# A selective-scan stage whose state input comes by broadcast DMA in place of selecting matmuls

## The chip, the cores and the metric

The kernel runs on one core of one Trainium2 chip. The metric is device time in microseconds of one execution; the times shown are those of three runs. One further execution was taken with the hardware profiler, and all rows below are from it. The engines are named as in the profile: PE is TensorE (PEld its weight loads), DVE is VectorE, ACT is ScalarE, POOL is GpSimd, SP is the engine that issues the DMAs.

## The reference

Two layers work on x, 8 sequences of 256 tokens with 128 features. Layer 0 adds grouped attention (16 heads, 4 key/value heads) and an expert layer with a softmax gate to x. Layer 1 adds a selective-scan block and a gated feed-forward block to the result, both from the same normalised input. The part that the change touches is the scan block:

```python
xz = x @ W_in
xs, z = (xz[..., :d_inner], xz[..., d_inner:])
...
xs = jax.nn.silu(xc.transpose(0, 2, 1))
dt = jax.nn.softplus(xs @ W_dt + b_dt)
Bs = xs @ W_x
A_exp = jnp.exp(A_log)
def step(h, inp):
    dt_t, Bs_t, x_t = inp
    h = h * jnp.exp(-A_exp[None] * dt_t[..., None]) + Bs_t[:, None, :]
    return (h, jnp.sum(h, axis=-1) + D * x_t)
...
y = ys.transpose(1, 0, 2) * jax.nn.silu(z)
return y @ W_out
```

There are 256 channels (two tiles of 128 partitions), 16 states per channel, and sequences of 256 tokens. For a state s, the state input Bs is one row of tokens that is the same for all channels; the decay differs by channel.

## The kernel before

Tokens lie along the free dimension in layer 1. The 2048 tokens are four groups (g = 0 to 3) of 512, each two sequences. Every engine has an order written out by hand (`ORDERS`): a list of pieces, each with the waits that it needs, which the engine runs from first to last. Layer 0 and layer 1 are interleaved in these lists.

For one group of layer 1 the pieces are:

- `x_transposes` and `x_out`: the normalised rows are transposed on TensorE and copied by ScalarE. `normalise` makes them on ScalarE in two passes per row tile (lines 997 and 1001).
- `x_in` (line 889): four matmuls, two for the x half and two for the z half, all into banks `pA` and `pB`. The z half waits for the convolution of the x half to leave the banks. `taps`, `conv` (line 1101, three multiply-adds per channel tile on VectorE), `gate_x` and `xm` (line 1092) make xs; `gate_z` and `zm` make z's gate.
- `start_acc` (line 988): ScalarE starts the accumulator with D times xs.
- `wx` (line 897): the state input, 16 rows three times over in 96 partitions. ScalarE copies it out twice (lines 1013 and 1014), and GpSimd's `split` turns it into three bf16 parts (lines 1178 to 1184).
- `b` (`b_row`, line 825): for each state one bf16 matmul with a selecting matrix brings its row to all 128 partitions, into a PSUM bank (bank 2 or 3).
- `dt` and `D` (`decay`, line 1047): ScalarE makes the step size, and for each state and channel tile the decay, into a ring of 31 SBUF tiles.
- `scan` (line 1125): for each state and channel tile one scan on VectorE. It reads the decay from SBUF and the state input from the PSUM bank and writes `hb`, eight SBUF tiles (four states by two channel tiles).
- `add` (line 1165): GpSimd adds each `hb` tile to the accumulator. `y` (line 1173) multiplies it by z's gate. A scan waits until the adds of four states before are done.
- `ffn`, `mul`, `second`, `gelu`, `third`, `hid`: the feed-forward block, TensorE and ScalarE with products on VectorE (lines 1081 and 1084).
- `out` (lines 925 and 927): the output rows of both blocks, into `pB`; `residual1` (line 1132) adds them to x, and SP writes the group out (line 805).

In all there are 4 groups by 16 states by 2 channel tiles: 128 scans and 128 adds. The scan reads its two operands like this (lines 1125 to 1127):

```python
eng.tensor_tensor_scan(hb[:, s % NPAIR, c, :],
                       da(n).rearrange("p b n -> p (b n)"),
                       b_bank(g, s)[:, :], 0.0, ALU.mult, ALU.add).then_inc(scan, 1)
```

In layer 0, `normalised` (line 631) is a `tensor_scalar` on VectorE; `G` on GpSimd (lines 680 to 699) is the gate's arithmetic on small tiles; `first_split` on VectorE (lines 639 to 645) splits the first sequence's queries and keys, and line 645 subtracts one SBUF tile from another. `warm` (line 445) is a matmul on constant data that keeps TensorE occupied.

Of the kernel before, what the change touches and what calls it, by code (L numbers as in the profile page):

```python
# [50 lines left out]
     ("alog", (CI, NS)), ("D", (CI,)), ("bdt", (CI,)), ("pick", (NS,))),  # L51
# [14 lines left out]
def settled(eng, sem, v):  # L66


    eng.wait_ge(sem, v)
# [3 lines left out]
    sync="""3*x_in constants0 head ffn_weights 3*put fetch stack 3*put fetch stack 3*put loads fetch 3*rows loads 3*put  # L73
        fetch 3*rows loads stack 2*put 2*rows put rows stack fetch loads 3*put 3*rows fetch stack 3*put 3*rows
        fetch stack 3*put 3*rows stack fetch 3*rows stack 3*rows 4*out landed""",
    tensor="""36*warm xn_transposes 4*warm project v_gate ffn_in 11*warm ffn_in 3*warm xn_transposes ffn_out 3*warm
        project ffn_in 2*S 2*warm xn_transposes S ffn_in S project S ffn_out 2*S 8*warm S xn_transposes warm S
        warm S 2*warm S warm S warm S 3*warm S 2*warm S 5*warm 2*S 4*warm max_rows warm S warm v_gate S warm S
        project warm 2*S 3*warm S A 2*warm S 2*A 2*S A S A S A pv S A S A ffn_in A S A S pv ffn_in A S A S
        max_rows ffn_out A S v_gate A S pv A S A S A S A pv S A S A heads A S A S pv A back xn_transposes A S A  # L80
        S proj_out project A S A S pv 2*S A ffn_in A S max_rows A pv v_gate ffn_in S A S A ffn_out S A S A pv S
        A S A heads S A S A pv xn_transposes A S A S back project S A S A pv proj_out S A S ffn_in 2*A S
        max_rows ffn_in S A S A pv v_gate S A S ffn_out A S A S pv A S A S heads A S A pv S A xn_transposes A S
        back project A S A S proj_out ffn_in 2*S A pv A S A ffn_in S A max_rows A ffn_out S A S v_gate pv S A S
        A pv S A S A heads A S A S pv A back A S xn_transposes proj_out A S A S project 2*A S pv S A S A pv S
        max_rows S ffn_in S A S v_gate A S ffn_in 2*S pv A S A S heads ffn_out S back A S A S proj_out S 2*A S
        pv 2*A 2*S A S A pv S 2*A max_rows ffn_in pv A 2*S A v_gate ffn_in A 2*S A ffn_out A S A S pv A S A S
        heads S A S A pv x_transposes A S A S back x_in S A S A pv proj_out ffn 2*A x_in max_rows A pv A ffn
        2*x_in 2*A ffn wx A pv ffn heads 2*step_in back b A second x_transposes proj_out A second b second A
        x_in b A x_in second b A pv A x_in A x_in A pv A b A wx A b step_in pv step_in b 2*A b 2*A b pv b second  # L90
        heads second 2*b 2*second b back third proj_out third b third b third b third b 2*third b x_transposes
        third b 2*x_in 2*ffn 2*b 2*x_in ffn wx b ffn b 2*out b step_in 2*second b 3*second 2*b second out b out
        second b x_transposes second b step_in b third b x_in third b 2*third x_in b 2*third b x_in 2*third b
        ffn b ffn b x_in wx b 2*ffn out b out step_in 2*out b 2*second b second b second b second b 2*second b
        second b step_in b third b third b 2*third b third b third b third b third b ffn b ffn out b out b 2*ffn
        b 2*out b 5*second 2*b 3*second b 3*third b 5*third 4*out""",
    scalar="""roots 3*deviation0 xn_out qk_out gate_exp 2*relu xn_out qk_out relu xn_out relu qk_out negated_maxima xn_out
        gate_exp qk_out 8*E relu 2*E relu E negated_maxima 7*E o_out 2*E gate_exp 3*E xn_out 2*E qk_out 3*E
        decay_rates negated_maxima relu 2*E relu 4*E o_out E gate_exp 3*E xn_out 2*E qk_out 3*E relu 2*E
        negated_maxima relu 5*E o_out 2*E gate_exp 3*E xn_out E qk_out 2*E relu 3*E relu E negated_maxima 4*E  # L100
        o_out 2*E gate_exp 4*E xn_out 2*E qk_out 2*E deviation E negated_maxima E relu 2*E normalise o_out relu
        normalise 2*E gate_exp 10*E negated_maxima relu 2*E relu 4*E o_out E gate_exp 3*E x_out 2*E taps 2*E sil
        2*E gate_x taps negated_maxima 2*E sil gate_x 2*gate_z 2*E start_acc sil b_in E o_out sil 2*dt D E 2*D E
        2*D x_out 3*D E D taps E D taps 2*D E 2*D E gate_x D E D gate_x E 2*gate_z E 2*D E start_acc b_in E 5*D
        dt 4*E 2*gelu dt o_out 8*D 2*gelu 7*D hid deviation hid 2*normalise x_out 2*hid D 2*taps 3*D sil gate_x
        sil gate_x gate_z start_acc gate_z D b_in 2*D 2*sil 15*D dt 4*D 4*gelu x_out D dt taps 5*D gate_x taps
        4*D 4*hid gate_x sil gate_z start_acc sil gate_z D b_in 2*D 2*sil 13*D dt 2*gelu 7*D 2*gelu dt 16*D
        4*hid D 2*sil 3*D 2*sil 11*D 4*gelu 4*hid""",
    vector="""ones clear 2*moments inverse normalised inverse moments inverse normalised v_out first_split gate_sum
        gate_norm normalised gated 2*M normalised 6*M normalised 10*M v_out 2*M gate_sum 2*M gate_norm 6*M gated  # L110
        11*M v_out 2*M heads 2*M gate_sum back_out gate_norm 2*M residual 2*M gated M normalised 6*M v_out 2*M
        heads 2*M gate_sum normalised 2*M gate_norm back_out 2*M gated residual 9*M v_out 2*M heads M gate_sum M
        gate_norm M normalised back_out gated 2*M residual 8*M v_out 2*M heads 2*M gate_sum back_out M gate_norm
        residual 2*M statistics 3*M gated inverse1 7*M v_out 2*M heads M back_out 2*M residual 2*M gate_sum 2*M
        gate_norm gated 8*M v_out 2*M heads 2*M gate_sum 2*M back_out gate_norm 2*M gated conv residual mul xm
        conv mul xm zm clear zm mul heads mul back_out scan residual 2*scan 2*conv xm scan zm xm scan zm 4*scan
        clear scan heads 2*scan back_out scan residual statistics 2*scan inverse1 4*scan 2*conv mul scan mul
        2*scan 2*mul 5*scan residual1 4*scan conv 2*scan conv 4*scan 2*mul 2*scan 2*mul 6*scan residual1 11*scan
        2*mul 2*scan 2*mul scan residual1 5*scan residual1""",
    gpsimd="""ones 3*biased 8*G 2*qk_split maxima_split 6*G qk_split 2*G constants maxima_split 8*G qk_split maxima_split  # L120
        8*G qk_split maxima_split 8*G qk_split maxima_split 8*G qk_split maxima_split 8*G maxima_split 8*G
        maxima_split split 10*add split 24*add 2*y 8*add split 22*add 2*y 10*add split 24*add y 3*add y 27*add
        2*y""",
# [22 lines left out]
def layer0(nc, sb, sem, banks, a, w, t, done):  # L146
# [24 lines left out]
    sb("spare", [P, 1106])  # L171
# [353 lines left out]
    def vector_pieces(eng):  # L525
        def ones(n):
            eng.memset(spark[:, :], 1.0).then_inc(spark_ok, 1)
            eng.memset(warm_in[:, :], 1.0).then_inc(warm_ok, 1)  # L528
            for p in range(2):
                eng.memset(v_sb[p][:, :, :, :], 0.0).then_inc(done["dv"], 1)  # L530
            eng.wait_ge(done["dv"], 2)
            for p in range(2):
                eng.memset(v_sb[p][:, :, :, VS + HD:VS + HD + 1], 1.0).then_inc(done["dv"], 1)

        def moments(k):
# [8 lines left out]
            eng.wait_ge(st_mv, 2 * k + 1)  # L544
            eng.tensor_scalar(t["veps"][:, lo:hi], mv[:, lo:hi, 1], LN_EPS, None, ALU.add).then_inc(st_mv, 1)
# [106 lines left out]
    def gpsimd_pieces(eng):  # L652
# [6 lines left out]
        def biased(k):  # L659
# [3 lines left out]
            TT(xb_sb[:, lo:hi, :], x_sb[:, lo:hi, :],  # L663
               bo_bc[:, :].rearrange("p (o n) -> p o n", o=1).broadcast_to([P, hi - lo, P]),
               ALU.add).then_inc(xb_ok, 1)
# [630 lines left out]
```

## Time and profile before

| | us |
|---|---|
| median of 3 runs | 415.81 (415.27 to 416.62) |
| the profiled execution | 415.58 |
| its span, first to last instruction | 413.7 |

| engine | busy us | share of the span |
|---|---|---|
| TensorE | 391.0 | 95% |
| VectorE | 313.3 | 76% |
| ScalarE | 311.5 | 75% |
| GpSimd | 239.5 | 58% |

The share of an engine is an average over stages that have different limits. TensorE's end times are modelled, because matmuls are pipelined, so a busy TensorE isn't TensorE at its peak. In a row of instruction groups stand line, engine, operation, output and inputs with their shapes, and the count; then the busy time, the mean in ns of one, and the idle time just before them with what ended most of it. In a timeline row stand start and length in us; a row with x6 is six instructions that follow each other. A scan or an add is one instruction over 128 partitions and 512 columns.

### The profile page before, as it was taken

What the parts mean: (1) busy time and instruction counts of PE and PEld (TensorE: products, weight loads), DVE (VectorE), ACT (ScalarE), POOL (GpSimd) and SP (SyncE); (2) the same over time, 40 slices, a digit from 0 to 9 for tenths busy, and PEclk for the clock granted to TensorE, in tenths of its full rate; (3) what the DMA queues carried; (4) which work ended last, traced back from release to release, by engine and by line L of the source; (5) the groups of instructions that cost most, each with busy time, mean ns of one, the idle gap of its engine ahead of it and who ended that gap; (6) DMA issues with size and microseconds to landing.
All of it is one profiled execution on the core that took longest, in us unless ns stands there. A gap on an engine that the chain in (4) does not pass through costs nothing.

```text
span 413.7 us, 5953 instructions
## 1 busy us (share of the span) xinstructions
PE 391.0 (95%) x1864; PEld 196.1 (47%) x1864; DVE 313.3 (76%) x521; ACT 311.5 (75%) x536; POOL 239.5 (58%) x276
## 2 busy tenths in 40 slices
PE   8998989999999999999878799899999999999996
PEld 6873534545454544334222344446444744465445
DVE  7557667887968778946967688987997799996620
ACT  1430357876868976769998999999999999999210
POOL 4333361514324111135488759698797999999740
PEclk9997889999999999999996899999999999999999
DMA  5189457176653703000000000000000000000000
GB/s 187 52 140 200 63 163 166 43 109 187 93 92 67 103 6 47 3 0 2 0 1 0 1 2 0 0 0 27 1 1 0 2 1 26 0 2 25 1 0 27
DMA packets 27679, 19.03 MB, mean 46 GB/s; under 512 B 2816, under 2 KB 26240, under 8 KB 27392
## 3 DMA queue, kind: packets, MB, share of 16 engines
q1 hardware_dynamic: 27648, 18.65, 22.1%
q8 instruction: 15, 0.25, 0.3%
q14 instruction: 16, 0.13, 0.1%
HBM read 13.46 MB, written 4.98 MB: 45 GB/s over the span
## 4 chain that ended last, share of the span: by engine, by line
PE 51%; ACT 29%; DVE 9%; issue 9%; POOL 0%; ACTq 0%; POOLq 0%; DVEq 0%
ACT da L1047 10%; PE bank L864 7%; PE bank L445 6%; PE bank L852 5%; PE bank L352 5%; DVE mx L558 4%; PE bank L391 4%; PE bank L323 4%; PE bank L337 3%; PE bank L383 3%; ACT L1047 3%; ACT pt L519 2%; PE bank L841 2%; DVE hb L1125 2%; PE bank L925 2%
## 5 line engine op out<-in xcount | busy, mean ns | idle before, releaser
L1165 POOL TENSOR_TENSOR acc<-acc,hb 128x512 f32<-128x512 f32 x128 | 158.2, 1273 | 37.1 <-DVE hb L1125 30.4
L1125 DVE TENSOR_TENSOR_SCAN hb<-da,bank 128x512 f32<-128x512 f32 x128 | 146.3, 1201 | 28.0 <-PE bank L825 20.2
L558 DVE TENSOR_REDUCE mx<-bank 128x2 f32<-128x512 f32 x128 | 82.8, 683 | 31.4 <-PE bank L323 26.0
L519 ACT ACTIVATE pt<-bank 128x512 f32<-128x512 f32 x128 | 71.6, 596 | 21.9 <-PE bank L337 21.3
L1047 ACT ACTIVATE da<-dt,nega 128x510 f32<-128x510 f32 x128 | 81.6, 710 | 0.2
L864 PE MATMUL bank<-gelu,ld 128*128 128x512 f32 x128 | 60.2, 608 | 3.1 <-ACT gelu L1028 3.1
L852 PE MATMUL bank<-sil,ld 128*128 128x512 f32 x128 | 59.2, 600 | 0.1
L337 PE MATMUL bank<-q_st,k_st 51*128 51x512 bf16 x128 | 44.3, 392 | 5.2 <-ACT pt L519 4.7
L323 PE MATMUL bank<-k_st,q_st 48*128 48x256 bf16 x256 | 45.1, 279 | 2.9 <-DVE mx L558 2.5
L864 PEld LDWEIGHTS bank<-gelu,ld 128*128 128x128 f32 x128 | 24.2, 192 | 31.6 <-issue 26.4
L852 PEld LDWEIGHTS bank<-sil,ld 128*128 128x128 f32 x128 | 24.1, 193 | 26.5 <-issue 24.6
L352 PE MATMUL bank<-pt,v_sb 128*32 128x512 f32 x256 | 35.8, 633 | 0.0
L445 PE MATMUL bank<-warm_in 128*128 128x256 bf16 x192 | 29.3, 307 | 1.4 <-DVE warm_in L528 1.4
L323 PEld LDWEIGHTS bank<-k_st,q_st 48*128 48x128 bf16 x256 | 16.7, 95 | 26.2 <-DVE mx L558 13.3
L337 PEld LDWEIGHTS bank<-q_st,k_st 51*128 51x128 bf16 x128 | 9.9, 93 | 32.8 <-ACT pt L519 19.3
L825 PE MATMUL bank<-b_parts,sel 96*128 96x512 bf16 x64 | 24.2, 388 | 0.7 <-ACT pt L519 0.7
L445 PEld LDWEIGHTS bank<-warm_in 128*128 128x128 bf16 x192 | 19.6, 109 | 9.1 <-issue 3.7
L1047 ACT ACT_TABLE_LOAD x17 | 21.8, 1283 | 0.3
L680 POOL TENSOR_TENSOR gd<-srt 128x16 f32<-128x16 f32 x8 | 1.7, 217 | 33.4 <-issue 30.6
L1035 ACT ACTIVATE gelu<-bank,ld 128x512 f32<-128x512 f32 x16 | 10.3, 687 | 12.8 <-PE bank L864 12.8
L1101 DVE SCALAR_TENSOR_TENSOR xc<-bank,ld,xc 128x510 f32<-128x510 f32 (+2 forms) x24 | 17.7, 744 | 2.5 <-ACT xc L960 1.9
L669 POOL TENSOR_TENSOR qk_parts<-qk,qk_parts 128x512 bf16<-128x512 f32 x7 | 8.1, 1158 | 18.0 <-ACT qk_parts L506 18.0
(145 smaller groups left out, 574.7 us busy)
## 6 DMA issues: line engine op xcount, KB each, us to landing
q_st<-q_scr SPq DMA_DIRECT2D x8, 384.0 KB, 6.6
q_st<-q_scr SPq DMA_DIRECT2D x15, 192.0 KB, 4.6
ld<-in_pack SPq DMA_DIRECT2D x2, 1024.0 KB, 5.9
q_scr<-qk_parts SPq DMA_DIRECT2D x8, 192.0 KB, 3.4
k_st<-k_scr SPq DMA_DIRECT2D x15, 96.0 KB, 5.3
q_scr<-qk_parts SPq DMA_DIRECT2D x8, 128.0 KB, 2.9
out<-x SPq DMA_DIRECT2D x4, 256.0 KB, 2.0
ld<-in_pack SPq DMA_DIRECT2D x1, 968.0 KB, 5.5
```

Of the source, the lines that this page charges most:

```text
L323: last = mm(s_bank[n % 2][:, j * T:(j + 1) * T], q_st[b % 2][0:ROWS, 2 * pair + j, q * P:(q + 1) * P], k_st[b % 2][0:ROWS, 2 * pair // G, ...
L337: mm(st(b, n)[:, :], k_st[b % 2][HALF:, kv, kt * P:(kt + 1) * P], q_st[b % 2][HALF:, h0:h0 + 2, :].rearrange("r h n -> r (h n)"), start=Tr ...
L352: last = mm(pv_bank[kv * VW:(kv + 1) * VW, :], v_sb[b % 2][:, kt, kv, at:at + VW], pt[:, (4 * grp + kv) % 8, :], start=(grp == 0), stop=(g ...
L445: last = mm(pv_bank[:, 0:256], warm_in[:, 0:P], warm_in[:, P:3 * P], start=True, stop=True)
L519: act(pt[:, n % 8, :], st(b, n)[:, :], ACT.Exp, scale=HD ** -0.5).then_inc(p_ok, 1)
L558: eng.tensor_reduce(mx[:, 2 * pair:2 * pair + 2, q], s_bank[n % 2][:, :].rearrange("p (h k) -> p h k", h=2), AX.X, ALU.max).then_inc(mx_ok, 1)
L825: mm(b_bank(g, s)[:, :], sel[:, s, :], b_parts[:, g % 2, :], start=True, stop=True).then_inc(b_ps, 1)
L852: last = mm(f_bank(g, c)[:, :], h1[:, k, c * P:(c + 1) * P], sil[:, k, :], start=(k == 0), stop=(k == KC - 1))
L864: last = mm(f_bank(g, c)[:, :], h2[:, k, c * P:(c + 1) * P], g2[:, k, :], start=(k == 0), stop=(k == KC - 1))
L1047: act(da(n)[:, :, 1:T], dt[:, g % 2, c, :].rearrange("p (b n) -> p b n", b=GB)[:, :, 1:T], ACT.Exp, scale=nega[:, c, s:s + 1]).then_inc(da ...
L1125: eng.tensor_tensor_scan(hb[:, s % NPAIR, c, :], da(n).rearrange("p b n -> p (b n)"), b_bank(g, s)[:, :], 0.0, ALU.mult, ALU.add).then_inc ...
L1165: TT(acc[:, g % 2, c, :], acc[:, g % 2, c, :], hb[:, s % NPAIR, c, :], ALU.add).then_inc(add_ok, 1)
```

## The change

The state input goes through DRAM. `wx` now makes 16 rows only, ScalarE copies them to `b_sb` once, SP stores them to a DRAM scratch (`b_put`), and for each two states SP fetches the two rows to all 128 partitions (`b_get`) into one of four SBUF slots `bt`. The scan reads the slot. The selecting matmuls, the three-part split on GpSimd and the selecting matrices are gone. z gets a bank of its own (bank 3) and pieces of its own (`z_in`), the output rows get bank 2. The accumulator's start moves from ScalarE to GpSimd. `normalise` is one pass. The variance's epsilon is given as a bias to the square root, where VectorE added it in an instruction of its own before. In layer 0, `normalised` becomes a `scalar_tensor_tensor` with a broadcast second operand, and the bias add on GpSimd is cut into pieces of two row tiles. The transposed input of layer 1 is kept for two groups in place of four, and the ring of decay tiles keeps its 31 tiles, cut differently. All five orders are written anew.

```diff
+        def b_put(g):
+            reached(eng, bx_ok, g, 1, 1)
+            eng.dma_start(b_scr[g:g + 1].rearrange("o s n -> (o s) n"), b_sb[:, :]).then_inc(b_put_ok, 16)
+
+        def b_get(n):
+            g, k = n // NBC, n % NBC
+            arrived, use, slot = chunk(n)
+            reached(eng, b_put_ok, g, 16, 16)
+            reached(eng, scan, 0, 1, CI * BROWS * (n + 1 - BSLOTS))
+            eng.dma_start(slot.rearrange("p s n -> p (s n)"),
+                          b_scr[g:g + 1, k * BROWS:(k + 1) * BROWS, :].rearrange("o s n -> o (s n)")
+                          .broadcast_to([P, BROWS * GT])).then_inc(arrived, 16)
...
         def scans(g, s):
-            reached(eng, b_ps, g, NS, s + 1)
+            arrived, use, slot = chunk((g * NS + s) // BROWS)
+            reached(eng, arrived, use, 16, 16)
             reached(eng, add_ok, g, 2 * NS, 2 * (s + 1 - NPAIR))
...
                 eng.tensor_tensor_scan(hb[:, s % NPAIR, c, :],
                                        da(n).rearrange("p b n -> p (b n)"),
-                                       b_bank(g, s)[:, :], 0.0, ALU.mult, ALU.add).then_inc(scan, 1)
+                                       slot[:, s % BROWS, :], 0.0, ALU.mult, ALU.add).then_inc(scan, 1)
...
+        def start_acc(g, c):
+            x_done(eng, g)
+            reached(eng, y_ok, g - 2, CI, CI)
...
+            eng.tensor_scalar(acc[:, g % 2, c, :], xs[:, g % 2, c, :], d[:, c:c + 1], None, ALU.mult).then_inc(acc_in, 1)
...
         def b_in(g):
-            act(b_parts[:, g % 2, :], pA[0:NPART * 32, :], ACT.Copy, scale=scale)
-            act(b_full[:, :], pA[0:NPART * 32, :], ACT.Copy, scale=scale).then_inc(bx_ok, 1)
+            reached(eng, b_put_ok, g - 1, 16, 16)
+            act(b_sb[:, :], pA[0:NS, :], ACT.Copy, scale=0.5 if g in TANH_GATES else 1.0).then_inc(bx_ok, 1)
...
         def out_rows(g, q):
-                if g + 2 < NG:
-                    z_done(eng, g + 2, 2)
-                else:
-                    reached(eng, dt_ok, NG - 1, CI, CI)
+                if g == 0:
+                    settled(eng, done["p_ok"], NB * NH)
                 reached(eng, o_ok, g - 1, 1, 1)
                 reached(eng, g3_ok, g, KC, KC)
                 reached(eng, y_ok, g, CI, CI)
...
-                act(xn[:, g % 2, q, :], x1[:, c, :], ACT.Identity, bias=nmean[:, c:c + 1]).then_inc(ctr_ok, 1)
...
-                last = act(xn[:, g % 2, q, :], xn[:, g % 2, q, :], ACT.Copy, scale=rstd[:, c:c + 1])
+                last = act(xn[:, g % 2, q, :], x1[:, c, :], ACT.Identity, bias=nmean[:, c:c + 1], scale=rstd[:, c:c + 1])
...
-                last = eng.tensor_scalar(xn[:, q, :], x_sb[:, c, :], mv[:, c, 0:1], rstd[:, c:c + 1],
-                                         ALU.subtract, ALU.mult)
+                last = eng.scalar_tensor_tensor(xn[:, q, :], x_sb[:, c, :], mv[:, c, 0:1],
+                                                rstd[:, c:c + 1].broadcast_to([P, P]), ALU.subtract, ALU.mult)
```

The parts of the new orders that matter from the scans on (ScalarE's list isn't shown; its counts of functions are told in the prediction):

```
vector   ... mul scan back_out scan mul residual 2*conv 3*scan 2*xm zm 3*scan zm scan clear 2*scan heads 3*scan back_out
         scan residual 2*scan statistics scan inverse1 3*scan 2*conv 2*mul scan 2*mul 12*scan conv scan residual1 scan
         conv 2*mul scan 2*mul 10*scan residual1 6*scan 2*mul 2*scan 2*mul 7*scan residual1 2*scan residual1
gpsimd   ... 2*start 10*add 2*start 24*add y 8*add y 2*add 2*start 26*add 2*y 2*add 2*start 27*add 2*y 29*add 2*y
sync     ... b_put 6*b_get b_put 9*b_get b_put 6*b_get out b_get b_put 5*b_get out 5*b_get 2*out landed
tensor   ... 2*third 2*ffn z_in wx 2*ffn step_in out 4*second out 4*second step_in out third out 7*third 2*ffn 2*out
         2*ffn 2*out 8*second 8*third 4*out
```

A `scan` piece is two scans (one state, both channel tiles); an `add`, a `start` and a `y` are one instruction each.

## Rows read from the trace of the kernel before

**Rows 1.** The core's span and its mean granted TensorE clock.

```profile
core 0: 413.7 us, clock 0.974
```

**Rows 2.** Busy time by stretch: us, PE, PEld, DVE, ACT, POOL, PEclk, DMA share, GB/s.

```profile
188.00:361.00 173.00, 162.78 (x503) 73.46 (x501) 147.94 (x162) 169.39 (x251) 144.04 (x121) 0.97 0.01 4
361.00:400.00 39.00, 38.22 (x129) 20.06 (x130) 27.00 (x27) 24.97 (x34) 32.70 (x27) 1.00 0.02 7
```

**Rows 3.** Groups of instructions by line, whole span.

```profile
L1165 POOL TENSOR_TENSOR acc<-acc,hb 128x512 f32<-128x512 f32 x128 | 158.2, 1273 | 37.1 <-DVE hb L1125 30.4 <-issue 6.4
L1125 DVE TENSOR_TENSOR_SCAN hb<-da,bank 128x512 f32<-128x512 f32 x128 | 146.3, 1201 | 28.0 <-PE bank L825 20.2 <-ACT da L1047 7.4
...
L825 PE MATMUL bank<-b_parts,sel 96*128 96x512 bf16 x64 | 24.2, 388 | 0.7 <-ACT pt L519 0.7
```

**Rows 4.** Tile hb: ns min/median/max, first and last start in us.

```profile
L1125 DVE TENSOR_TENSOR_SCAN hb<-da,bank x128: 1169/1196/1222, 188.4 to 396.5; 128x512 f32<-128x512 f32 x128
L1165 POOL TENSOR_TENSOR acc<-acc,hb x128: 1257/1272/1297, 189.7 to 397.9; 128x512 f32<-128x512 f32 x128
```

**Rows 5.** Timeline of VectorE, 196 to 206.6 us.

```profile
197.10 4.50 DVE L1101 SCALAR_TENSOR_TENSOR xc<-bank,ld,xc 128x510 f32<-128x510 f32 x6
201.52 0.68 DVE L1092 SCALAR_TENSOR_TENSOR xs<-xs,xc 128x512 f32<-128x512 f32 x1
...
205.25 1.22 DVE L1092 SCALAR_TENSOR_TENSOR xs<-xs,xc 128x512 f32<-128x512 f32 x1
```

**Rows 6.** Timeline of GpSimd, 196 to 208 us.

```profile
196.15 2.51 POOL L1165 TENSOR_TENSOR acc<-acc,hb 128x512 f32<-128x512 f32 x2 [0.81 <-DVE hb L1125]
...
203.41 2.51 POOL L1165 TENSOR_TENSOR acc<-acc,hb 128x512 f32<-128x512 f32 x2 [4.75 <-DVE hb L1125]
```

**Rows 7.** Timeline of all engines near 16 us, and line 684's lengths in ns.

```profile
16.16 0.69 DVE L645 TENSOR_TENSOR qk_parts<-qk_rest,qk_parts 128x512 bf16<-128x512 f32 x1
...
16.43 0.49 POOL L684 TENSOR_TENSOR g<-gex 128x8 f32<-128x8 f32 x1 [1.43 <-ACT gex L512]
...
L684 POOL TENSOR_TENSOR g<-gex x8: 201/202/492, 16.4 to 159.0; 128x8 f32<-128x8 f32 x8
```

**Rows 8.** Groups of GpSimd's instructions by line and form, 160 us to the end.

```profile
L1173 POOL TENSOR_TENSOR y<-acc,zs 128x512 f32<-128x512 f32 x8 | 10.0, 1271 | 0.0
...
L1180 POOL CAST b_mid<-b_rest 96x512 bf16<-96x512 f32 x4 | 2.4, 607 | 0.3
```

**Rows 9.** DMA issues: count, KB each, median us from issue to landing.

```profile
q_st<-q_scr SPq DMA_DIRECT2D x15, 192.0 KB, 4.6
ld<-in_pack SPq DMA_DIRECT2D x2, 1024.0 KB, 5.9
...
w<-in_w SPq DMA_DIRECT2D x1, 512.0 KB, 5.8
...
k_scr<-qk_parts SPq DMA_DIRECT2D x8, 32.0 KB, 2.7
```

**Rows 10.** Timeline of ScalarE, 178.3 to 186.3 us.

```profile
178.93 0.58 ACT L1014 ACTIVATE b_full<-bank 96x512 f32<-96x512 f32 x1
```

**Rows 11.** Timeline of all engines, 398 us to the end.

```profile
399.14 2.50 POOL L1173 TENSOR_TENSOR y<-acc,zs 128x512 f32<-128x512 f32 x2
...
404.88 1.13 PE L925 MATMUL bank<-ld,gelu 128*128 128x128 f32 x8 [0.94 <-issue]
...
409.87 0.61 PE L927 MATMUL bank<-ld,y 128*128 128x128 f32 x4
```

**Rows 12.** Busy time by stretch (columns as in rows 2).

```profile
234.00:238.00 4.00, 3.29 (x4) 1.31 (x5) 1.62 (x2) 3.97 (x7) 3.22 (x3) 0.62 0.00 0
```

**Rows 13.** Groups of ScalarE's instructions by line, 188 to 361 us.

```profile
L1047 ACT ACT_TABLE_LOAD x13 | 16.7, 1283 | 0.2
...
L988 ACT ACTIVATE acc<-xs,ld 128x512 f32<-128x512 f32 x4 | 2.7, 720 | 0.0
...
L1001 ACT ACTIVATE xn<-xn,rstd 128x128 f32<-128x128 f32 x8 | 2.5, 393 | 0.0
```

More of the change, by code:

```diff
@@ L72 @@
 ORDERS = dict(
[L73 to L119, printed above, removed]
@@ L120 @@
-    gpsimd="""ones 3*biased 8*G 2*qk_split maxima_split 6*G qk_split 2*G constants maxima_split 8*G qk_split maxima_split
+    sync="""constants0 2*x_in head ffn_weights x_in 3*put fetch stack 3*put stack put fetch 2*put loads fetch 3*rows
+        loads 3*put fetch 3*rows loads stack put rows 2*put 2*rows stack fetch loads 3*put 3*rows fetch stack
+        3*put 3*rows stack fetch 3*put fetch 3*rows stack 3*rows stack 3*rows b_put 6*b_get b_put 9*b_get b_put
+        6*b_get out b_get b_put 5*b_get out 5*b_get 2*out landed""",
@@ L121 @@
+    gpsimd="""ones 3*biased 8*G 2*qk_split maxima_split 7*G qk_split G constants maxima_split 8*G qk_split maxima_split
         8*G qk_split maxima_split 8*G qk_split maxima_split 8*G qk_split maxima_split 8*G maxima_split 8*G
-        maxima_split split 10*add split 24*add 2*y 8*add split 22*add 2*y 10*add split 24*add y 3*add y 27*add
-        2*y""",
+        maxima_split 2*start 10*add 2*start 24*add y 8*add y 2*add 2*start 26*add 2*y 2*add 2*start 27*add 2*y
+        29*add 2*y""",
 )
@@ L662, in biased @@
             eng.wait_ge(ld_cst, 16)
-            TT(xb_sb[:, lo:hi, :], x_sb[:, lo:hi, :],
-               bo_bc[:, :].rearrange("p (o n) -> p o n", o=1).broadcast_to([P, hi - lo, P]),
-               ALU.add).then_inc(xb_ok, 1)
+            for c in range(lo, hi, TPB):
+                last = TT(xb_sb[:, c:c + TPB, :], x_sb[:, c:c + TPB, :],
+                          bo_bc[:, :].rearrange("p (o n) -> p o n", o=1).broadcast_to([P, TPB, P]), ALU.add)
+            last.then_inc(xb_ok, 1)
         def qk_split(b):
@@ L806, in out_dma @@
                           x1[:, g * GTT:(g + 1) * GTT, :]).then_inc(out_ok, 16)
+        def b_put(g):
[9 more added lines that the diff above has]
+                          .broadcast_to([P, BROWS * GT])).then_inc(arrived, 16)
         def landed(n):
             eng.wait_ge(out_ok, 16 * NG)
-        return dict(out=out_dma, landed=landed)
+        return dict(out=out_dma, b_put=b_put, b_get=b_get, landed=landed)
     def tensor_pieces(eng):
         mm = eng.matmul
-        def b_row(g, s):
-            if s == 0:
-                reached(eng, bsp, g, NBS, NBS)
-                if g == 0:
-                    settled(eng, done["p_ok"], (NB - 1) * NH)
-            if g == 0 and s == NB1:
-                settled(eng, done["p_ok"], NB * NH)
-            reached(eng, scan, g, 2 * NS, 2 * s if g == 0 and s < NB1 else 2 * (s - 1))
-            mm(b_bank(g, s)[:, :], sel[:, s, :], b_parts[:, g % 2, :], start=True, stop=True).then_inc(b_ps, 1)
         def ffn_first(g, c):
@@ L942, in deviation @@
             lo, hi = PARTS[part]
-            eng.wait_ge(st_ok, 3 * part + 2)
-            act(std[:, lo:hi], t["veps"][:, lo:hi], ACT.Sqrt).then_inc(sd_ok, 1)
+            eng.wait_ge(st_ok, part + 1)
+            act(std[:, lo:hi], mv[:, lo:hi, 1], ACT.Sqrt, bias=t["eps"][:, 0:1]).then_inc(sd_ok, 1)
         def ffn_silu(g, c):
@@ L1109, in statistics @@
             last.then_inc(st_ok, 1)
-            eng.wait_ge(st_ok, 3 * part + 1)
-            eng.tensor_scalar(t["veps"][:, lo:hi], mv[:, lo:hi, 1], LN_EPS, None, ALU.add).then_inc(st_ok, 1)
-            eng.tensor_scalar(nmean[:, lo:hi], mv[:, lo:hi, 0], -1.0, None, ALU.mult).then_inc(st_ok, 1)
         def inverse(part):
@@ L1198, in constants @@
                               ALU.mult).then_inc(i_pool, 1)
-        return dict(constants=constants, split=split, add=lambda n: add(n // (2 * NS), n % (2 * NS)),
+        return dict(constants=constants, start=lambda n: start_acc(n // CI, n % CI), add=lambda n: add(n // (2 * NS), n % (2 * NS)),
                     y=lambda n: gated(n // CI, n % CI))
@@ L1270 @@
     eye = _np.eye(P, dtype=_np.float32)
-    pick = _np.tile(_np.eye(32, NS, dtype=_np.float32), (P // 32, 1))
     parts = dict(
```

211 lines of the change are left out of this document (115 added, 96 removed).

## The prediction

> **What bounds the kernel now.** The runs shown have a median of 415.81 us; the profiled execution took 415.58 us, 0.2 us less, of which 413.7 us are its span [rows 1] and 1.9 us lie around it. All sums below are made against 415.6 us.
>
> I read the stretches first [rows 2]. From 188 to 361 us, the scan stage, ScalarE is busy 169 of 173 us: it sets the pace, with TensorE (163 us) close behind. From 361 us to the end it is TensorE, which runs the last group's feed-forward layers (38.2 of 39 us) while VectorE has 27 instructions left. VectorE and GpSimd have slack in the scan stage (148 and 144 of 173 us), and that slack exists because they work at the same time: 128 scans of 1.20 us on VectorE and 128 adds of 1.27 us on GpSimd [rows 3] overlap. Their sum, 317 us, is far more than the 211 us from the first scan at 188.4 to the end of the last add at 399.2 us [rows 4]. So the question to put to any edit of these two instructions is whether they can still overlap.
>
> **The scan's second operand.** Today the scan reads the decay from SBUF and the state input from a PSUM bank. The change makes the state input an SBUF tile, so the scan has two SBUF inputs. The trace holds few VectorE instructions with two SBUF inputs that meet a GpSimd instruction, and they are the rows to look at. Line 1092 multiplies two SBUF tiles: at 201.52 us, with GpSimd idle, it takes 0.68 us; at 205.25 us it takes 1.22 us [rows 5]. GpSimd was in two adds from 203.41 to 205.92 us [rows 6]. The slow one ended at 206.47, 0.54 us after the adds: it stood still until they were over, and only the 0.14 us of its fixed part passed meanwhile. The six taps of line 1101 just before, with one SBUF and one PSUM input, ran beside adds at 0.75 us each [rows 5], and all 128 scans, also from PSUM, lie between 1.17 and 1.22 us [rows 4]. The other way round, line 645 (two SBUF inputs, 0.69 us from 16.16) made GpSimd's line 684 take 0.49 us in place of its usual 0.20; it ended 0.07 us after line 645 did [rows 7], so 0.13 us of its fixed part had passed. In both directions the one waits for the whole of the other.
>
> From these rows a scan that waits for an add costs 1.20 − 0.14 = 1.06 us after it, and an add that waits for a scan 1.27 − 0.13 = 1.14 us. A pair takes 2.20 us by turns, and 128 pairs 281.6 us, against 211 us now.
>
> The Trainium skill, "SBUF — State Buffer", section "Who interferes with whom", says that a VectorE instruction with two SBUF inputs contends with a GpSimd instruction that reads SBUF and that the loser blocks for the whole of the winner. By whole instructions a pair would be 2.47 us, the sum 35 us longer; the two events above hide the fixed part, so the rows' 2.20 is taken and the other kept as the upper end. No row shows a scan itself in that position.
>
> **What else takes a turn.** If scans and GpSimd's instructions take turns, so do others. From the first scan on: six of the eight y multiplications (line 1173, 1.27 us, 1.14 after a wait), 6.8 us; six of the eight new starts of the accumulator, which move from ScalarE to GpSimd. The trace has no such GpSimd instruction; bounds are the one-input cast of line 1180 (0.61 us) and the two-input add (1.27 us) [rows 8]; the form is the cast's, so 0.47 us after a wait, 2.8 us. Two x multiplications at 0.54 us, 1.1 us. Together 10.7 us.
>
> **VectorE's work outside the turns** is only partly covered, because VectorE runs in order: while it does taps, feed-forward products or residuals, GpSimd finishes the one add that is waiting, 1.14 us, and is then short of scans. In the new order eight such blocks after the first scan are longer than an add: product, residual and two convolutions 6.8 us, two convolutions and two products 6.0, one and two 3.7, one convolution 2.25, and four pairs of products at 1.5 (a convolution is three taps at 0.75 us [rows 5], a product of the feed-forward is the same form and taken at the same). They sum to 24.75 us; less eight adds, 15.6 us are added. Shorter blocks vanish behind an add.
>
> **The DMA in place of the matmuls.** 64 selecting matmuls (24 us of TensorE's busy time [rows 3]) and GpSimd's four splits per group go; 32 fetches of 512 KB and four 32 KB stores come, all on SP's queue. The fetch shape isn't in the trace; 1024 KB landed in 5.9 us, 512 KB of weights in 5.8, 192 KB in short runs in 4.6 [rows 9]. Taking 5.8 us, three fetches ahead of their use, it is hidden behind the 8.8 us that two state rows take at 2.20 us a pair. If that cover went, it would be the second rival. Only the first chunk can lie on the path: state input ready at 179.5 us [rows 10], a 32 KB store 2.7, the fetch 5.8, both issues 0.8: 188.8, against the first scan at 188.4, so nothing to speak of. SP's output DMAs now stand behind fetches that wait for scans; the last one follows all scans anyway.
>
> **ScalarE and TensorE** lose work that no longer sets the end. By the new order ScalarE loads its table 44 times in place of 47 (counting changes of function reproduces the 47), does half of each normalise, one copy less of the state input and no accumulator start. Output rows of a group wait for its y, with the next group's feed-forward behind them in TensorE's queue. At the new pace y of groups 1 and 2, which stand behind 70 and 99 adds, come near 350 and 420 us; the decays of the pairs that follow lie ready, and the last group's feed-forward (some 35 us) still ends before the last add. Layer 0 keeps its order but for small moves: TensorE reaches the first transposes after 38 warm pieces in place of 36, which cover the earlier constants, the statistics without their extra step and the bias add in eight pieces. I take the first scan where it was, 188.4 us, with 6 us either way. The normalisation of layer 0 on VectorE becomes a form with two SBUF inputs; it waited for GpSimd before and may still: nothing.
>
> **The sum.** 188.4 + 281.6 + 10.7 + 15.6 = 496.3 us, the end of the last add. Then both y, 2.5 us, and from the first output row to the end what it is now, 413.7 − 404.9 = 8.8 us [rows 11]. These output matmuls (404.88 to 410.48, 5.6 us) now follow an idle TensorE: between 234 and 238 us, where it was busy for 3.3 of 4 us, the granted clock was 0.62 [rows 12], that is mostly the 1.2 GHz level; at that level all the way they would take 5.6 us more, at 2.4 GHz nothing, and I take 4. Span 511.6 us, and 1.9 around it: **513.5 us**, 24% longer.
>
> **Rivals.** First, the scan is not held up (two events, neither a scan, are thin evidence, and a scan takes 1.20 us over the same 512 columns as a product of 0.68, which may leave room between its reads). Then the change pays where it was bound, on ScalarE between 188 and 361 us: three table loads at 1.28, 3.8 us; six accumulator starts at 0.72, 4.3; the second half of eight normalise pieces 2.5 [rows 13]; three copies at 0.58 [rows 10], 1.7: 12.3 us, and with about 1 us of selecting matmuls from the last stretch 402.3 us, between 395 and 412. It decides if in the new profile scans keep 1.20 and adds 1.27 us while they overlap. For it: nothing in the trace has a scan against an add with this operand. Against it: both events, without an exception. Chance 0.08.
>
> Second, DMA supply: all 128 partitions fetch the same 4 KB of DRAM. At the rate of the 192 KB fetches, 42 KB per us, a chunk would take 12.3 us and 32 of them 393 us, more than the turns' 308; the end would be near 188 + 393 + 9 (the last chunk's scans and adds) + 15 + 2 = 607 us. It decides once a chunk takes over 8.8 us at full queue. For it: that row. Against it: those transfers are made of short runs, and 1024 KB packs came at 174 KB per us. Chance 0.04.
>
> Third, the change doesn't do what it says, because the waiting merely moves: something else still ends later, so that the time stays. With ScalarE and TensorE both shorter I see no such work. Chance 0.01.
>
> **How the numbers follow.** The forecast has 0.87. Low end: an add that waits keeps only 1.27 − 0.20 = 1.07 us (all of line 684's length is fixed part), pairs of 2.13 us, 272.6 us; the work outside the turns wholly covered; first scan at 182.4; no loss of clock: 182.4 + 272.6 + 10 + 2.5 + 8.8 + 1.9 = 478 us. High end: pairs of 2.47 us, 316.6 us; each add 0.1 us late because it isn't waiting yet (the first add started at 189.7, 0.1 us after the first scan's 188.4 + 1.20 [rows 4]), 13 us; nothing covered, 24.75; the other users at full length with 1.27 us starts, 16.6; first scan at 194.4; the slow tail 16.9; and 1.9: 584 us. All at once is unlikely; without the late adds it is 571, and I stop at 570. From 478 to 570 us lie some 0.80 of the chances. About 0.3% (1.2 us) is what a measurement of this kernel can tell from no change. Faster 0.08, same 0.01, slower 0.91.
>
> **What the new profile would show.** If I am right: scans and adds alternate, or one of them is recorded at about twice its length; their busy times together fill the stretch from the first scan to the last add, some 308 us; ScalarE and TensorE are idle for long stretches there; fetches land before they are waited for. Wrong in size: pairs off 2.2 us, or long waits of the adds for decays or of the scans for a fetch. Wrong in kind: scans of 1.20 us that overlap with adds of 1.27 us, and a span near 400 us.

## The result, and the profile after

The changed kernel takes 505.62 us (median of 4 runs, 504.65 to 507.91) against 415.73 us (4 runs, 415.27 to 416.62) in the same comparison: a ratio of 1.217, 95% interval 1.212 to 1.221. That is some 90 us slower. The profiled execution took 505.37 us, 503.6 of them its span. Some ranges below are wide because the kernel before comes at two granted clocks: over three of the comparisons, 14 of its 53 executions had 0.983 to 0.988 and took some 411.5 us (410.5 to 414.0), the others had 0.979 or less and took some 416.

The first view is again the core's row; it answers to [rows 1].

```profile
core 0: 503.6 us, clock 0.892
```

The mean clock fell from 0.974 to 0.892. TensorE has far more idle time than before, as the next view shows; that goes with the lower clock and says nothing yet of the cause. The stretch from the first scan to the end of the last add shows who is busy (columns as in [rows 2]: length, PE, PEld, DVE, ACT, POOL, PEclk, DMA share, GB/s):

```profile
185.00:490.00 305.00, 208.12 (x569) 95.86 (x569) 285.60 (x190) 183.85 (x261) 281.81 (x140) 0.84 0.15 52
```

Before, ScalarE and TensorE filled the scan stage and VectorE and GpSimd had slack. Now it is the other way round: VectorE is recorded busy for 286 of 305 us and GpSimd for 282, while ScalarE is busy for 184 and TensorE for 208. The groups of the page say with what (columns as in [rows 3]):

```profile
L1161 POOL TENSOR_TENSOR acc<-acc,hb 128x512 f32<-128x512 f32 x128 | 261.9, 2080 | 31.7 <-DVE hb L1114 31.7
L1114 DVE TENSOR_TENSOR_SCAN hb<-da,bt 128x512 f32<-128x512 f32 x128 | 253.6, 2046 | 8.9 <-ACT da L1035 8.9
```

Both instructions have the shapes that they had before. The mean add went from 1273 to 2080 ns and the mean scan from 1201 to 2046. The view of the tile hb shows the spread (min/median/max in ns, first and last start), against [rows 4]:

```profile
L1114 DVE TENSOR_TENSOR_SCAN hb<-da,bt x128: 1193/2218/2235, 185.0 to 485.8; 128x512 f32<-128x512 f32 x128
L1161 POOL TENSOR_TENSOR acc<-acc,hb x128: 1256/2179/2253, 186.3 to 489.0; 128x512 f32<-128x512 f32 x128
```

The minimum is the old length: a scan that meets no add, or that starts before it, still takes 1.19 us. The median scan is 2.22 us, which is its own 1.2 us and most of an add. The instructions themselves aren't slower; each long record holds the time in which the other engine was served, as the experiments below show. The chain of waits gives the step of the alternation from starts alone, whatever a record includes:

```profile
379.43 0.09 POOL acc L1161
379.51 2.06 issue
381.58 0.09 POOL acc L1161
381.67 2.07 issue
383.74 0.08 POOL acc L1161
...
422.32 0.09 POOL acc L1161
```

"issue" is time in which the engine waited for nothing that the profile shows. From 379.43 to 422.32 us are 20 steps, (422.32 − 379.43)/20 = 2.145 us for one scan and one add.

The new transfers are far from the path (count, KB each, median us from issue to landing):

```profile
bt<-b_scr SPq DMA_DIRECT2D x32, 512.0 KB, 3.7
b_scr<-b_sb SPq DMA_DIRECT2D x4, 32.0 KB, 1.6
```

No scan waited for a fetch: the only releaser in the scans' group above is the decay. The end of the timeline answers to [rows 11]:

```profile
490.25 2.48 POOL L1169 TENSOR_TENSOR y<-acc,zs 128x512 f32<-128x512 f32 x2
...
492.94 2.05 PE L926 MATMUL bank<-ld,gelu 128*128 128x128 f32 x8 [13.14 <-issue]
...
499.82 0.61 PE L928 MATMUL bank<-ld,y 128*128 128x128 f32 x4
```

From the first output row to the end of the last it is 7.5 us (492.94 to 500.43), against 5.6 before.

### The profile page after: what moved, and what is told of

Same layout as the page of the kernel before. It is cut to its first block and busy times, and to the rows that moved or that the text cites. A ratio compares the mean times of both kernels' runs of the same rounds, so it can differ in the third digit from the quotient of the medians.

```text
span 503.6 us, 5846 instructions
## 1 busy us (share of the span) xinstructions
PE 393.4 (78%) x1800; PEld 197.3 (39%) x1800; DVE 416.6 (83%) x517; ACT 299.3 (59%) x505; POOL 343.4 (68%) x268
## 5 line engine op out<-in xcount | busy, mean ns | idle before, releaser
L1161 POOL TENSOR_TENSOR acc<-acc,hb 128x512 f32<-128x512 f32 x128 | 261.9, 2080 | 31.7 <-DVE hb L1114 31.7
L1114 DVE TENSOR_TENSOR_SCAN hb<-da,bt 128x512 f32<-128x512 f32 x128 | 253.6, 2046 | 8.9 <-ACT da L1035 8.9
L926 PE MATMUL bank<-ld,gelu 128*128 128x128 f32 x128 | 21.1, 319 | 39.6 <-issue 39.6
L837 PE MATMUL bank<-xnT,ld 128*128 128x512 f32 x32 | 19.5, 696 | 24.7 <-ACT gelu L1023 21.3
L926 PEld LDWEIGHTS bank<-ld,gelu 128*128 128x128 f32 x128 | 20.1, 232 | 45.8 <-issue 45.8
L351 PE MATMUL bank<-pt,v_sb 128*32 128x512 f32 x256 | 34.5, 618 | 0.0
L444 PE MATMUL bank<-warm_in 128*128 128x256 bf16 x192 | 27.4, 288 | 1.4 <-DVE warm_in L528 1.4
L956 ACT ACTIVATE sil<-bank,ld 128x512 f32<-128x512 f32 x12 | 7.7, 684 | 28.6 <-PE bank L838 28.6
L702 POOL TENSOR_TENSOR m_parts<-negm,m_parts 32x128 bf16<-32x128 f32 x8 | 3.3, 417 | 28.8 <-ACT negm L487 28.8
```

The costliest lines, as they stand in the source:

```text
L351: last = mm(pv_bank[kv * VW:(kv + 1) * VW, :], v_sb[b % 2][:, kt, kv, at:at + VW], pt[:, (4 * grp + kv) % 8, :], start=(grp == 0), stop=(g ...
L444: last = mm(pv_bank[:, 0:256], warm_in[:, 0:P], warm_in[:, P:3 * P], start=True, stop=True)
L926: mm(out_bank[:, r], g3[:, k, r], w3[:, k, :], start=(k == 0), stop=False)
L1114: eng.tensor_tensor_scan(hb[:, s % NPAIR, c, :], da(n).rearrange("p b n -> p (b n)"), slot[:, s % BROWS, :], 0.0, ALU.mult, ALU.add).then_ ...
L1161: TT(acc[:, g % 2, c, :], acc[:, g % 2, c, :], hb[:, s % NPAIR, c, :], ALU.add).then_inc(add_ok, 1)
```

## The experiments

**The second operand alone.** The kernel before, whose scans read a resident weight tile in SBUF in place of the bank. A wait for that tile's load is added; nothing else is changed.

```diff
         def scans(g, s):
+            eng.wait_ge(done["ld"][0], 16)
...
-                                       b_bank(g, s)[:, :], 0.0, ALU.mult, ALU.add).then_inc(scan, 1)
+                                       win[:, :], 0.0, ALU.mult, ALU.add).then_inc(scan, 1)
```

> The kernel before with one edit: the scan's second operand is a weight tile in SBUF in place of the selected PSUM bank (the state input is left out of the scans; all matmuls, splits, orders and waits stay). Theory, scans and adds take turns: a pair takes 2.15 us as after the change, the stage from first scan to last add about 128 x 2.15 + 25 = 300 us, the time 495 to 515 us, scans and adds recorded near 2.1 us. Rival, the fetches by DMA or the new orders cost the time: no change, 416 us, scans 1.2 us.

Measured: 498.65 us (494.89 to 502.42), ratio 1.197 [1.188, 1.206]. Its tile hb:

```profile
L1126 DVE TENSOR_TENSOR_SCAN hb<-da,ld x128: 1193/2218/2295, 183.7 to 473.1; 128x512 f32<-128x512 f32 x128
L1166 POOL TENSOR_TENSOR acc<-acc,hb x128: 1254/2180/2196, 185.0 to 478.8; 128x512 f32<-128x512 f32 x128
```

The medians, 2218 and 2180 ns, are within a nanosecond those of the changed kernel, with no fetch, no scratch and none of the new orders in it. One operand of one instruction costs about 82 us of the 90 (0.197 × 416). The other 8 us belong to the rest of the change and weren't taken apart.

**The fetches.** The changed kernel with 4 of its 32 fetches.

```diff
         def b_get(n):
...
+            if n >= BSLOTS:
+                return
...
-            reached(eng, arrived, use, 16, 16)
+            reached(eng, arrived, 0, 16, 16)
```

> The kernel after with only the first 4 of the 32 fetches (the scans read stale state input after that): 14 MB of DMA traffic and 28 waits for it are gone. Theory: nothing of the time is in the fetches, 502 to 507 us. Rival, fetch supply or the traffic's writes into SBUF slow scans or adds: at least 20 us faster.

Measured: 505.63 us (505.19 to 507.62), against 505.62 with all fetches. Taking 14 MB of transfers away (28 of 512 KB) changes nothing; the rival of the DMA supply is out.

**A GpSimd that only writes.** The changed kernel, with a memset for each add.

```diff
-            TT(acc[:, g % 2, c, :], acc[:, g % 2, c, :], hb[:, s % NPAIR, c, :], ALU.add).then_inc(add_ok, 1)
+            eng.memset(acc[:, g % 2, c, :], 1.0).then_inc(add_ok, 1)
```

> The kernel after with each of the 128 adds replaced by a memset of the accumulator (the sum over states is left out): same queue, waits and output tile, but GpSimd no longer reads SBUF there. Theory, a scan with two SBUF inputs waits for a GpSimd instruction that reads SBUF: scans return to 1.2 us, the time to what the rest of the change is worth, 395 to 412 us. Rival, the scan from SBUF is slow by itself or the fetches disturb it: scans stay near 2.1 us and the time at 500 or more.

Measured: 399.15 us (398.52 to 400.01), ratio 0.961 [0.955, 0.966].

```profile
L1114 DVE TENSOR_TENSOR_SCAN hb<-da,bt x128: 1192/1199/2267, 184.6 to 378.1; 128x512 f32<-128x512 f32 x128
...
L1161 POOL MEMSET acc<- 128x512 f32 x128 | 67.1, 525 | 114.3 <-DVE hb L1114 114.3
```

The scan with its two SBUF operands is back at 1.20 us (median 1199). So the operand is slow only in company. But this memset takes 0.525 us where an add takes 1.27, so that the run changes two things: GpSimd reads nothing, and its instruction is shorter. Two more runs separate them.

**A long write.** The same with a memset of both halves of the accumulator (and with the waits that this needs).

```diff
-            reached(eng, add_ok, g, 2 * NS, n - 1)
-            TT(acc[:, g % 2, c, :], acc[:, g % 2, c, :], hb[:, s % NPAIR, c, :], ALU.add).then_inc(add_ok, 1)
+            reached(eng, add_ok, g, 2 * NS, n)
+            eng.memset(acc[:, g % 2, :, :], 1.0).then_inc(add_ok, 1)
```

> The changed kernel, with each of the 128 adds replaced by a memset of both halves of the accumulator (1024 columns, so the sum of the states is left out). The write-only run before used 0.525 us memsets and so also made GpSimd shorter than an add of 1.27 us. Here the instruction is about 0.9 to 1.1 us long, near an add, but still reads nothing. Theory (a scan with two SBUF operands waits for what GpSimd reads, and for nothing that it only writes): scans stay near 1.20 us, and the time stays between 398 and 412 us. Rival (what counts is how long GpSimd occupies the memory, reading or writing): pairs of 1.20 + 1.0 - 0.14 = about 2.06 us, 128 of them 264 us, and a time near 490 us.

Measured: 400.0 us (399.22 to 401.31), ratio 0.962 [0.960, 0.965].

```profile
L1114 DVE TENSOR_TENSOR_SCAN hb<-da,bt x128: 1193/1200/2228, 185.7 to 380.4; 128x512 f32<-128x512 f32 x128
...
L1161 POOL MEMSET acc<- 128x1024 f32 x128 | 121.9, 952 | 61.8 <-DVE hb L1114 59.8
...
L1169 POOL TENSOR_TENSOR y<-acc,zs 128x512 f32<-128x512 f32 x8 | 13.9, 1748 | 0.1
```

A GpSimd instruction of 0.95 us that only writes holds no scan up. The four scans of over 2 us that remain (max 2228) all lie beside y, which still reads two tiles: y has a mean of 1748 ns against 1271 before [rows 8].

**The shorter GpSimd by itself.** The same memset in the kernel before.

```diff
-            TT(acc[:, g % 2, c, :], acc[:, g % 2, c, :], hb[:, s % NPAIR, c, :], ALU.add).then_inc(add_ok, 1)
+            eng.memset(acc[:, g % 2, c, :], 1.0).then_inc(add_ok, 1)
```

> The kernel before, with each of the 128 adds replaced by a memset of its half of the accumulator (0.525 us, reads nothing; the sum of the states is left out). It tells how much of the 17 us that the write-only run of the changed kernel gained over the kernel before comes from the shorter GpSimd instruction alone. If GpSimd is no bound in the kernel before (ScalarE and TensorE pace the scan stage, the last adds and y are only a tail), it is worth the last adds' difference and little more: 413 to 416 us. Rival (GpSimd is a joint bound, as the run without the selecting matmuls and with the lean ScalarE suggests): 400 to 409 us.

Measured: 415.54 us (411.4 to 416.65) against 415.66, ratio 0.997 [0.993, 1.001]. From 188 to 361 us:

```profile
188.00:361.00 173.00, 162.78 (x506) 73.47 (x504) 147.33 (x161) 170.29 (x251) 73.01 (x124) 0.98 0.01 4
```

GpSimd's busy time falls from 144 to 73 us and nothing else moves: GpSimd was no bound. So the 16 us by which the long-write run beats the kernel before don't come from a shorter GpSimd instruction, as far as the old order can tell, but from the rest of the change. Part of them goes with the clock: all executions of the long-write run had 0.983 to 0.987, and against those of the kernel before at 0.983 to 0.988 (some 411.5 us) the gain is 11 to 12 us.

**One input in place of two.** The changed kernel, whose adds become copies of hb, so that GpSimd still reads, but for half as long.

```diff
-            TT(acc[:, g % 2, c, :], acc[:, g % 2, c, :], hb[:, s % NPAIR, c, :], ALU.add).then_inc(add_ok, 1)
+            eng.tensor_copy(acc[:, g % 2, c, :], hb[:, s % NPAIR, c, :]).then_inc(add_ok, 1)
```

> The kernel after with each add replaced by a one-input copy of the scan's tile into the accumulator (the sum over states is left out): GpSimd still reads SBUF, for half as long (0.61 us alone, by the cast of the kernel before). Theory, the wait is as long as the other engine's instruction: a pair takes 1.06 + 0.48 = 1.54 us, so scans are recorded near 1.6 us in place of 2.1, 128 pairs take 197 us, and the time falls to 400 to 425 us, where ScalarE and TensorE set the pace again. Rival, any read by GpSimd costs the scan a fixed penalty: scans stay near 2.1 us and the time above 490.

Measured: 427.51 us (426.41 to 429.8), ratio 1.029 [1.024, 1.034].

```profile
L1114 DVE TENSOR_TENSOR_SCAN hb<-da,bt x128: 1192/1559/2222, 186.3 to 414.0; 128x512 f32<-128x512 f32 x128
L1161 POOL COPY acc<-hb x128: 603/1537/1620, 187.6 to 415.9; 128x512 f32<-128x512 f32 x128
```

A copy alone takes 603 ns, and the median scan beside it 1559. So the wait is no fixed penalty: it shrinks with the other instruction. The total came 2.5 us above the range given; why wasn't followed up.

**Half of the scans.** The kernel before, in which the scans of the second channel tile alone read SBUF.

```diff
-                                       b_bank(g, s)[:, :], 0.0, ALU.mult, ALU.add).then_inc(scan, 1)
+                                       win[:, :] if c == 1 else b_bank(g, s)[:, :], 0.0, ALU.mult, ALU.add).then_inc(scan, 1)
```

> The kernel before with the SBUF operand for one of the two channel tiles alone (those scans leave the state input out): 64 scans have two SBUF inputs, 64 have one. Theory, by turns for the 64 alone: per state GpSimd needs two adds (1.27 + 1.14) and stands still for one scan (1.06), 3.47 us, 64 states 222 us, then y and the end: 425 to 445 us; scans of the one tile near 2.1 us, of the other 1.2. Rival, the cost is in proportion to the scans: half of 82 us, 457 us.

Measured: 444.85 us (443.97 to 445.3), ratio 1.070 [1.064, 1.075], at the upper edge of the range. Its tile hb, two rounds of four scans on VectorE, and GpSimd's adds beside them:

```profile
L1166 POOL TENSOR_TENSOR acc<-acc,hb x128: 1253/1274/2278, 190.1 to 429.6; 128x512 f32<-128x512 f32 x128
L1126 DVE TENSOR_TENSOR_SCAN hb<-da,bank x64: 1160/1206/1222, 188.7 to 424.8; 128x512 f32<-128x512 f32 x64
L1126 DVE TENSOR_TENSOR_SCAN hb<-da,ld x64: 1191/1404/2315, 189.8 to 425.9; 128x512 f32<-128x512 f32 x64
...
289.04 1.22 DVE L1126 TENSOR_TENSOR_SCAN hb<-da,bank 128x512 f32<-128x512 f32 x1 [0.69 <-POOL acc L1166]
290.18 2.20 DVE L1126 TENSOR_TENSOR_SCAN hb<-da,ld 128x512 f32<-128x512 f32 x1
292.30 1.19 DVE L1126 TENSOR_TENSOR_SCAN hb<-da,bank 128x512 f32<-128x512 f32 x1
293.41 1.19 DVE L1126 TENSOR_TENSOR_SCAN hb<-da,ld 128x512 f32<-128x512 f32 x1
295.86 1.22 DVE L1126 TENSOR_TENSOR_SCAN hb<-da,bank 128x512 f32<-128x512 f32 x1 [1.26 <-POOL acc L1166]
297.00 2.19 DVE L1126 TENSOR_TENSOR_SCAN hb<-da,ld 128x512 f32<-128x512 f32 x1
...
288.80 18.30 POOL L1166 TENSOR_TENSOR acc<-acc,hb 128x512 f32<-128x512 f32 x11
```

All 64 scans from the bank lie between 1160 and 1222 ns in the same program; only the others reach 2.2 us. In these rounds every second one of those keeps 1.19 us, but not because GpSimd is idle: its 11 adds follow each other without a gap at 18.30/11 = 1.66 us each. There it is the add that waited (adds reach 2278 ns). From 289.04 to 295.86 us are two states, 3.41 us each, where the expectation had 3.47 by turns. Half of the operands costs 29 of the 82 us.

**What relief is worth.** Three runs on the kernel before take load off ScalarE and TensorE. The first moves the accumulator's start to GpSimd and makes the normalisation of layer 1 one pass, as the change does (the entries in the orders and the waits that go with it aren't shown):

```diff
-                act(acc[:, g % 2, c, :], xs[:, g % 2, c, :], ACT.Copy, scale=d[:, c:c + 1]).then_inc(acc_in, 1)
...
+            eng.tensor_scalar(acc[:, g % 2, c, :], xs[:, g % 2, c, :], d[:, c:c + 1], None, ALU.mult).then_inc(acc_in, 1)
...
-                last = act(xn[:, g % 2, q, :], xn[:, g % 2, q, :], ACT.Copy, scale=rstd[:, c:c + 1])
+                last = act(xn[:, g % 2, q, :], x1[:, c, :], ACT.Identity, bias=nmean[:, c:c + 1], scale=rstd[:, c:c + 1])
```

> The kernel before with two parts of the change alone: normalise in one pass and the accumulator's start on GpSimd; scans still read PSUM, matmuls and splits stay. Theory, ScalarE sets the pace between 188 and 361 us: it loses six starts at 0.72 and eight passes at 0.39 us there, 7 us, so 407 to 411 us. Rival, the freed time on ScalarE is taken up by waits for TensorE: 414 to 416 us. GpSimd gains 8 instructions of about 0.6 us, which take no turn since the scan has one SBUF input.

Measured: 414.69 us (409.91 to 415.89) against 416.13, ratio 0.996 [0.991, 1.000]. Missed: this relief of ScalarE is worth about 1.4 us, and the interval reaches no change.

```profile
188.00:361.00 173.00, 163.70 (x509) 74.57 (x510) 149.88 (x162) 167.77 (x240) 152.44 (x127) 0.98 0.01 4
```

The second cuts 62 of the 64 selecting matmuls to 8 columns:

```diff
-            mm(b_bank(g, s)[:, :], sel[:, s, :], b_parts[:, g % 2, :], start=True, stop=True).then_inc(b_ps, 1)
+            n = GT if g == 0 and s in (0, NB1) else 8
+            mm(b_bank(g, s)[:, 0:n], sel[:, s, :], b_parts[:, g % 2, 0:n], start=True, stop=True).then_inc(b_ps, 1)
```

> The kernel before with 62 of the 64 selecting matmuls cut to 8 columns (the scans read stale state input); waits, banks, GpSimd's splits and all else stay. It shows what TensorE's part in the selecting matmuls is worth by itself. If TensorE, not ScalarE, is the bound beside which the rest of the change gains: 62 x about 0.2 us = 12 us less work, 403 to 410 us. If ScalarE alone sets the pace: 413 to 416 us.

Measured: 414.07 us (410.56 to 414.97) against 415.93, ratio 0.995 [0.991, 0.999], inside the range given (413 to 416) for a ScalarE that paces alone: TensorE's relief is worth about 2 us. The third has both edits.

> Both: normalise in one pass, accumulator start on GpSimd, and the selecting matmuls cut to 8 columns, in the kernel before. If the two engines stand close behind each other, so that relief of one alone gives little, both together give more than the sum of 1.5 us and e6's gain: 398 to 406 us. If the gains only add: 1.5 us below e6.

Measured: 413.52 us (409.18 to 416.23), ratio 0.994 [0.989, 1.000]. Of the two outcomes that were named, the larger gain (398 to 406 us) is out: both reliefs together bring 2.4 us, at most the sum of the two. In the first of the three runs ScalarE is still busy for 168 of the 173 us. Over the whole span it has 6.9 us less to do (304.6 us busy against 311.5), yet the span is 0.9 us shorter (412.8 against 413.7): the rest became waiting. So these reliefs, in the old order, don't explain the 16 us of the long-write run. What is left for them is the new order with the own banks for z and the output rows, or these together with the reliefs; as bank 2 and bank 3 are the ones that the state input used to fill, this wasn't tried apart, and stays open.

## Why the prediction was right

**The turns.** This was the step that decided, and the runs show it from four sides: the operand alone brings the loss; a GpSimd that only writes takes it away; a shorter read makes it shorter; within one program only the scans with the SBUF operand suffer. The prediction took 2.20 us a pair from two events, neither of them a scan; 2.145 us was measured. If every pair takes that, they take 128 × 2.145 = 274.6 us, against the 281.6 of the sum. It sits close to the low bound of 2.13, where the fixed part that runs beside the other instruction is 0.2 us of the add.

The Trainium skill, "SBUF — State Buffer", section "Who interferes with whom", says that a VectorE instruction with two SBUF inputs contends with a GpSimd instruction that reads SBUF and not with one that only writes. The long-write run agrees (scans at 1200 ns beside writes of 952). In its section "SBUF: two separate sides" the page also has the loser wait for the whole instruction. The trace doesn't agree with that: it would be 2.47 us a pair, and the measured 2.145 decides.

**The stage.** Predicted 188.4 to 496.3 us, 307.9; measured 185.0 to 490.25, 305.3. Beside the pairs' 274.6 us that leaves 30.7, against a predicted 26.3. That sum hides two terms that failed. The first is the accumulator's start on GpSimd, taken at 0.47 us after a wait, from the cast of the same form:

```profile
L1153 POOL TENSOR_SCALAR acc<-xs,ld 128x512 f32<-128x512 f32 x4 | 6.2, 1562 | 0.1
```

It takes 1.56 us, more than a two-input add and so outside both of the bounds that were named (0.61 and 1.27). That is its own length and no waiting, for the first of the three relief runs, whose scans read the bank, has the same:

```profile
L1152 POOL TENSOR_SCALAR acc<-xs,ld 128x512 f32<-128x512 f32 x4 | 6.2, 1560 | 0.2
```

Six in the stage occupy GpSimd for about 9.4 us in place of 2.8. But a start doesn't take a full turn, as was assumed. The first two lines are from the changed kernel, the last two from the long-write run:

```profile
296.89 1.56 POOL L1153 TENSOR_SCALAR acc<-xs,ld 128x512 f32<-128x512 f32 x1
296.96 1.68 DVE L1114 TENSOR_TENSOR_SCAN hb<-da,bt 128x512 f32<-128x512 f32 x1 [1.78 <-ACT da L1035]
...
207.26 1.57 POOL L1153 TENSOR_SCALAR acc<-xs,d_half 128x512 f32<-128x512 f32 x1 [1.59 <-DVE xs L1080]
207.97 1.22 DVE L1114 TENSOR_TENSOR_SCAN hb<-da,bt 128x512 f32<-128x512 f32 x1
```

A scan that begins with a start takes 1.68 us and not the 2.55 that a wait for the whole start would make (1.56 + 1.06 less the 0.07 that it began later); one that begins 0.71 us into it isn't held up. Taking off the 1.06 us of a scan that has waited, the first was let through 0.7 us after the start began. That is an estimate, from one scan here and two like it near 213 us in the changed kernel (1.34 and 1.64 us long); no run was made for it. So 9.4 us is an upper bound of what the starts cost.

The second term is a wait that the prediction said would not be there ("the decays of the pairs that follow lie ready"). Adds at the new pace make y late; ScalarE's gate of z for the group after next waits for y, since z has two buffers; and ScalarE's decays are queued behind that gate. The timeline of ScalarE and then of VectorE:

```profile
285.01 1.28 ACT L971 ACT_TABLE_LOAD   x1 [7.71 <-POOL y L1169]
...
289.88 1.33 ACT L1035 ACTIVATE da<-dt,nega 128x510 f32<-128x510 f32 x2
```

```profile
287.51 1.41 DVE L1072 SCALAR_TENSOR_TENSOR sil<-bank,ld,sil 128x512 f32<-128x512 f32 x2 [2.90 <-ACT sil L956]
290.73 2.34 DVE L1114 TENSOR_TENSOR_SCAN hb<-da,bt 128x512 f32<-128x512 f32 x2 [1.81 <-ACT da L1035]
```

y of group 0 ended at 284.9 us; ScalarE had stood still for 7.7, and VectorE then waited for its products and decays. In all the scans waited 8.9 us for decays. With starts at 9.4 or less and y and x as priced (6.8 and 1.1), 13.4 us or more are left for these waits and for VectorE's work outside the turns together, where 15.6 were taken for the work alone. How they divide wasn't measured. That the stage came within 3 us of its forecast, with terms wrong on both sides, is in part luck.

**The start and the end.** The first scan came at 185.0, 3.4 us before the forecast, within its 6 us; why wasn't followed up. The loss of clock in the output rows is 7.5 − 5.6 = 1.9 us, where 4 were taken. TensorE ran no matmul from 480 to 490 us, and the granted clock was 0.50, the 1.2 GHz level, from 492.90 to 495.85 us and 0.89 from there to 500.50, so that only the first part of the rows was slow:

```profile
492.90:495.85 2.95, 2.91 (x14) 2.94 (x14) 0.00 (x0) 0.00 (x0) 0.00 (x0) 0.50 0.00 0
495.85:500.50 4.65, 4.58 (x36) 4.38 (x35) 0.04 (x1) 0.00 (x0) 0.00 (x0) 0.89 0.00 0
```

From the first output row to the end of the span are 503.6 − 492.9 = 10.7 us, against 8.8 + 4. Start, stage and end all came out shorter than forecast, and together they make the 8 us by which the forecast was high: 3.4 for the start, 2.6 for the stage (pairs 7.0 less, the rest 4.4 more), and 2.0 for the end (15.3 us of span behind the last add were forecast, 503.6 − 490.25 = 13.35 measured).

**DMA.** Hidden, as said: the fetch takes 3.7 us, where 5.8 were taken and 8.8 were to spare. The rival at 607 us rested on the rate of short runs of bytes, and the broadcast of a 4 KB row isn't like them.

**The other side.** The first rival, 402 us (395 to 412), was priced near what the changed kernel takes once nothing but y holds its scans up: 400 us, with adds that only write. That the number fits is in part luck, since of its 12.3 us of relief on ScalarE the two parts that were tried in the old order (4.3 and 2.5 us) gave 1.4 us.

## What to carry to other kernels

Before an operand moves from PSUM to SBUF, count the SBUF inputs of the VectorE instruction that reads it, and look at what GpSimd reads meanwhile, and for how long: two engines that overlapped can become one that takes turns, and the price is the sum of their times less a fixed part. One or two instructions in the old trace that are unexpectedly twice as long beside GpSimd are enough to see it coming. And relief of the busiest engine can be worth little: here 1.4 us of the 6.8 us of ScalarE's work that was taken away. Price it by a run, not by its busy time.

## What the runs showed that was not expected

GpSimd's multiplication of one tile by a value per partition took 1.56 us for 128 × 512, the add of two tiles 1.27, a copy 0.60 and a memset 0.525; by the cast and the add it had been put between 0.6 and 1.27. A two-input add holds a scan up for most of its length, a start of 1.56 us only for about half of it (by the estimate above). In the half-operand run the loss was 29 us, where half of the whole was 41, so the cost isn't proportional to the number of such scans. A reason that fits, but wasn't shown: in the kernel before, a state takes 3.3 us on average (211 us for 64), which is set by other engines, and the first waits use up that slack.
